# Router logits of a mixture-of-experts layer: standing router weights, tokens through four column groups, and a transpose back

## The reference

```python
h = tok(x, weight, weighted_sum)                      # (32, 512, 256)
h = h + attn(layernorm(h), ...)                       # ctx @ Wo + bo is its last step
xf = layernorm(h).reshape(-1, 256)
logits = xf @ router_w + router_b                     # router_w: (256, 8)
scores = softmax(logits, axis=-1)
G, idx = top_k(scores.T, 512)                         # per expert
...                                                   # experts on the chosen tokens, added into h
```

## Time and profile before

| what | value |
|---|---|
| median of 3 runs | 4833.21 us (4829.96 to 4833.23) |
| the profiled execution's own time | 4812.72 us |
| its span | 4811.0 us |
| mean granted TensorE clock | 0.959 of full |
| PE busy | 4480.2 us, 93% |
| DVE busy | 3479.2 us, 72% |
| ACT busy | 2664.6 us, 55% |
| POOL busy | 1843.0 us, 38% |

### The profile page before, as it was taken

The page is one execution under the profiler, slowest core; times in us unless marked ns, Lnnn a source line. Parts: engine busy times, 40 slices in busy tenths (PEclk is TensorE's granted clock), DMA queues, the critical chain, the costliest instruction groups (busy, mean ns, idle before and its releaser), DMA issues. The chain is left out here.

```text
span 4811.0 us, 92103 instructions
## 1 busy us (share of the span) xinstructions
PE 4480.2 (93%) x30324; PEld 3229.2 (67%) x30324; DVE 3479.2 (72%) x9091; ACT 2664.6 (55%) x5075; POOL 1843.0 (38%) x4431
## 2 busy tenths in 40 slices
PE   6999999699999999999999999999999997892699
PEld 5777777367776767766777766777767675772666
DVE  3333333288889888888899988889889896876411
ACT  1222222267777777777777777777777773440121
POOL 1222222244444444444444444444444442330032
PEclk9999999799999999999999999999999998995599
DMA  5888888899999999999999999999999995662033
GB/s 169 279 282 280 281 278 283 270 398 391 396 392 393 393 391 394 391 392 393 393 392 396 394 392 390 394 390 396 391 391 393 393 385 185 219 213 70 7 94 83
DMA packets 684020, 1540.36 MB, mean 320 GB/s; under 512 B 50211, under 2 KB 286163, under 8 KB 683475
## 3 DMA queue, kind: packets, MB, share of 16 engines
q1 hardware_dynamic: 674646, 1523.26, 85.7%
q0 software_dynamic: 6144, 8.52, 1.0%
q10 hardware_dynamic: 2816, 3.41, 0.3%
HBM read 753.82 MB, written 781.21 MB: 319 GB/s over the span
## 5 line engine op out<-in xcount | busy, mean ns | idle before, releaser
L984 ACT ACTIVATE a_probsT<-a_ps_m_t 128x512 f32<-128x512 f32 x2048 | 1228.4, 607 | 826.4 <-PE a_ps_m_t L924 826.4
L1046 DVE CUSTOM_DVE_ANT_1 a_scored<-a_ps_m_s,a_bias 128x512 f32<-128x512 f32 x2048 | 1397.7, 682 | 294.8 <-PE a_ps_m_s L915 283.1
L924 PE MATMUL a_ps_m_t<-a_ident,a_scored 128*128 128x128 f32 x8192 | 1256.6, 276 | 0.5 <-ACT a_probsT L984 0.5
L924 PEld LDWEIGHTS a_ps_m_t<-a_ident,a_scored 128*128 128x128 f32 x8192 | 934.7, 141 | 433.2 <-DVE a_scored L1053 431.2
L978 ACT ACTIVATE a_skew_in<-a_ps_m_tab 128x512 f32<-128x512 f32 x2048 | 1128.1, 617 | 67.7 <-PE a_ps_m_tab L901 36.1
L1053 DVE TENSOR_SCALAR a_scored<-a_scored,a_top_of 128x512 f32<-128x512 f32 x2048 | 1039.7, 527 | 0.0
L870 POOL TENSOR_SCALAR_AFFINE_SELECT a_bias<-a_bias 128x128 f32<-128x128 f32 (+2 forms) x2560 | 974.3, 407 | 35.1
L861 POOL COPY a_bias<-a_high 128x128 f32<-128x128 f32 (+1 forms) x1024 | 359.3, 380 | 1571.5 <-DMA a_bias<-d_skew 1571.5
L915 PE MATMUL a_ps_m_s<-a_ident,a_bias 128*128 128x128 f32 x5120 | 894.7, 273 | 0.0
L915 PEld LDWEIGHTS a_ps_m_s<-a_ident,a_bias 128*128 128x128 f32 x5120 | 688.7, 141 | 177.7 <-issue 1.0
L901 PE MATMUL a_ps_m_tab<-a_tabs,a_stack 128*128 128x256 bf16 x4096 | 709.3, 276 | 78.2 <-DMA a_ident<-in_ident 30.7
(11 more groups left out here) (195 smaller groups left out, 3658.2 us busy)
## 6 DMA issues: line engine op xcount, KB each, us to landing
d_skew<-a_skew_in SPq DMA_DIRECT2D x512, 1024.0 KB, 8.5
a_bias<-d_skew SPq DMA_DIRECT2D x512, 896.0 KB, 9.5
a_stack<-d_stack SPq DMA_DIRECT2D x256, 512.0 KB, 9.9
p_xt<-in_xT SPq DMA_DIRECT2D x31, 2048.0 KB, 10.4
d_stack<-p_extra SPq DMA_DIRECT2D x64, 512.0 KB, 3.2
d_ctx<-a_ctx_sb SPq DMA_DIRECT2D x128, 256.0 KB, 8.8
d_stack<-p_part_q SPq DMA_DIRECT2D x64, 384.0 KB, 2.8
d_stack<-p_part_k SPq DMA_DIRECT2D x64, 384.0 KB, 3.4
```

The lines of the kernel that those rows point to most:

```text
L924: mm = pe.transpose(m_t[:, k % 2, t * P:(t + 1) * P], scored[:, hh % SCORED, t, k * P:(k + 1) * P], ident[:])
L984: nc.scalar.activation(turned_at(hh // GH, hh % GH, k), m_t[:, k % 2], ACT.Exp, scale=SCALE).then_inc(turned, 1)
L1046: nc.vector.tensor_tensor_reduce(split(scored[:, hh % SCORED, t]), split(m_s[:, t % 2]), extra, 1.0, -3.0e38, ALU.add, ALU.max, top_of[:, ...
```

## The change

The router's weights are padded to 32 columns (`wr` is [128, 2, 32], cleared by POOL, and the load fills the first 8), and stand as weights; the tokens of one tile of 128 run through. The product of token tile t goes to the output partitions 32t to 32t+31, so that the logits come out with the experts on partitions and the tokens along the row (`by_expert`, 128x128). ACT copies that to SBUF (`logitsT`), PE transposes it (`turn_back`) into `by_token`, and DVE reads 8 of each 32 columns of it. `route(n)` moves ahead of `widen(n+3, 1)`, and `turn_back(n)` stands behind it.

```diff
@@ -1084,7 +1084,8 @@
 
     BUFS = 4
     ident, wo = sb("ident", [P, P]), sb("wo", [P, HC, H])
-    bo_row, wr, br_row = sb("bo_row", [P, H]), sb("wr", [P, HC, NE]), sb("br_row", [P, NE])
+    bo_row, wr, br_row = sb("bo_row", [P, H]), sb("wr", [P, HC, P // QT]), sb("br_row", [P, NE])
+    logitsT = sb("logitsT", [P, P])
     heads_f, heads = sb("heads_f", [P, OCT, HC, P]), sb("heads", [P, OCT, HC, P], BF16)
     minus_half = sb("minus_half", [P, QT])
     sums, inverse = sb("sums", [P, B // OCT, S]), sb("inverse", [P, S])
@@ -1096,17 +1097,18 @@
     xg, xT = sb("xg", [P, BUFS, QT, XG]), sb("xT", [P, HC, S])
     logits, expd = sb("logits", [P, QT, NE]), sb("expd", [P, QT, NE])
     top_of, total, share = sb("top_of", [P, QT]), sb("total", [P, QT]), sb("share", [P, QT])
-    m_o, m_turn, m_r = ps("m_o", [P, 2, QT, H]), ps("m_turn", [P, HC, S]), ps("m_r", [P, QT, NE])
+    m_o, m_turn, m_r = ps("m_o", [P, 2, QT, H]), ps("m_turn", [P, HC, S]), ps("m_r", [P, 2, QT, P // QT])
     m_share = ps("m_share", [P, S])
-    half_set, heads_in, heads_kept, wo_in, const_in = (
-        sem("o_" + n) for n in ("half_set", "heads_in", "heads_kept", "wo_in", "const_in"))
+    half_set, wr_cleared, heads_in, heads_kept, wo_in, const_in = (
+        sem("o_" + n) for n in ("half_set", "wr_cleared", "heads_in", "heads_kept", "wo_in", "const_in"))
     sums_in = [sem(f"o_sums_in{o}") for o in range(B // OCT)]
     c_loaded, h_loaded, h_stored, xg_stored = ([sem(f"o_{n}{u}") for u in range(BUFS)]
                                                for n in ("c_loaded", "h_loaded", "h_stored", "xg_stored"))
     (inverted, cut, share_done, scaled, o_done, h_added, h_done, st_done, mo_done, ve_done, rs_done, centred,
-     xn_done, turn_done, turned, r_done, soft, exp_done, xg_done) = (sem("o_" + n) for n in (
+     xn_done, turn_done, turned, routed, kept, r_done, soft, exp_done, xg_done) = (sem("o_" + n) for n in (
          "inverted", "cut", "share_done", "scaled", "o_done", "h_added", "h_done", "st_done", "mo_done", "ve_done",
-         "rs_done", "centred", "xn_done", "turn_done", "turned", "r_done", "soft", "exp_done", "xg_done"))
+         "rs_done", "centred", "xn_done", "turn_done", "turned", "routed", "kept", "r_done", "soft", "exp_done", "xg_done"))
+    by_expert, by_token = (m_r[:, k].rearrange("p t e -> p (t e)") for k in range(2))
     SOFT = 6
     CUTS = 5
     octets = B // OCT
@@ -1144,7 +1146,9 @@
             load_h(0)
             load_context(2)
             load_h(1)
-            for dst, src in ((ident[:], io["ident"]), (wr[:], io["router_w"].rearrange("(c p) o -> p c o", p=P)),
+            sp.wait_ge(wr_cleared, 1)
+            for dst, src in ((ident[:], io["ident"]),
+                             (wr[:, :, 0:NE], io["router_w"].rearrange("(c p) o -> p c o", p=P)),
                              (br_row[:], io["router_b"].partition_broadcast(P))):
                 sp.dma_start(dst, src).then_inc(const_in, 16)
             load_h(2)
@@ -1172,6 +1176,7 @@
 
         @block.gpsimd
         def _(pool):
+            nc.gpsimd.memset(wr[:], 0.0).then_inc(wr_cleared, 1)
             nc.gpsimd.memset(minus_half[:], -0.5).then_inc(half_set, 1)
             pool.wait_ge(half_set, 1)
             pool.wait_ge(wo_in, 32)
@@ -1230,11 +1235,16 @@
             def route(n):
                 after(pe, turned, HC * (n + 1))
                 after(pe, soft, SOFT * n)
-                for t in range(QT):
-                    for c in range(HC):
-                        mm = pe.matmul(m_r[:, t], xT[:, c, t * P:(t + 1) * P], wr[:, c], start=(c == 0),
-                                       stop=(c == HC - 1))
-                mm.then_inc(r_done, 1)
+                for c in range(HC):
+                    for t in range(QT):
+                        mm = pe.matmul(by_expert[t * (P // QT):(t + 1) * (P // QT)], wr[:, c],
+                                       xT[:, c, t * P:(t + 1) * P], start=(c == 0), stop=(c == HC - 1),
+                                       skip_group_check=True)
+                mm.then_inc(routed, 1)
+
+            def turn_back(n):
+                after(pe, kept, n + 1)
+                pe.transpose(by_token, logitsT[:], ident[:]).then_inc(r_done, 1)
 
             pe.wait_ge(heads_kept, 1)
             for n in range(3):
@@ -1251,9 +1261,10 @@
                     widen(n + 3, 0)
                 if n + 2 < B:
                     project_out(n + 2, n % 2)
+                route(n)
                 if n + 3 < B:
                     widen(n + 3, 1)
-                route(n)
+                turn_back(n)
 
         @block.scalar
         def _(act):
@@ -1278,8 +1289,11 @@
             for n in range(B):
                 for c in range(HC):
                     act.wait_ge(turn_done, HC * n + c + 1)
-                    after(act, r_done, n)
+                    after(act, routed, n)
                     nc.scalar.activation(xT[:, c], m_turn[:, c], ACT.Identity).then_inc(turned, 1)
+                act.wait_ge(routed, n + 1)
+                after(act, r_done, n)
+                nc.scalar.activation(logitsT[:], by_expert, ACT.Identity).then_inc(kept, 1)
                 act.wait_ge(soft, SOFT * n + 3)
                 nc.scalar.activation(expd[:], logits[:], ACT.Exp).then_inc(exp_done, 1)
                 if n + 2 < B:
@@ -1337,7 +1351,7 @@
                     after(dve, soft, SOFT * n + k)
 
                 after(dve, r_done, n + 1)
-                step(nc.vector.tensor_tensor(logits[:], m_r[:], br_row[:].unsqueeze(1).to_broadcast([P, QT, NE]),
+                step(nc.vector.tensor_tensor(logits[:], m_r[:, 1, :, 0:NE], br_row[:].unsqueeze(1).to_broadcast([P, QT, NE]),
                                              ALU.add), 1)
                 step(nc.vector.tensor_reduce(top_of[:], logits[:], AX.X, ALU.max), 2)
                 step(nc.vector.tensor_tensor(logits[:], logits[:], top_of[:].unsqueeze(2).to_broadcast([P, QT, NE]),
```

## The result

The changed kernel takes 4810.8 us in the median of 5 runs, the one before 4833.2 us: the ratio is 0.9956, with an interval of 0.9946 to 0.9967. That is 21 us or 0.44% faster (the two medians themselves lie 22.5 us apart). The two profiled executions, however, differ by only 7.7 us (4812.7 and 4805.0), close to the 6.6 us of the forecast's sum. One later execution of the changed kernel ran in a slower state of the chip (5246.6 us at a mean granted clock of 0.83) and one of before took 17821 us; neither is used for a reading.

A forecast was written before the change was run, and what follows sets the result against it. DVE and PE's 8.39 us ring bounds the output stage's batches, with 15.0 us lost to the clock. Ring 0, clock -3.9, tail -2.7 make -6.6 us: 4806, carried to the median as 4826.6 us, range 4816 to 4839.

The forecast's parts named there:

- the clock's term: Output stage's steady batches: half-clock losses of 15.0 us would become 11.1, a term of -3.9 us.
- the carrying over: Whole kernel: -6.6 us gave 4806 for the profiled execution; the median's 20 us above it was added, giving 4826.6.
- the floor of 239.3 us: Output stage's 27 steady batches without clock loss: 226.5 us at 8.39 each plus 12.8 us of DVE's in six batches.
- the tail: Last three batches, little overlap, half clock: the router product is on the path; the stage ends 2.7 us sooner.
- rival 1: The clock holds in the output stage: -13.8 us, about 4819; with no fall left -17.7, 4815.5. Chance 0.35.
- The ring of 8.39 us: Full-clock batch: share product, projection, DVE's addition of h, statistics and scaling set 8.39 us; the change shortens it by 0.
- The product's size: Router product on PE: its slot falls from 1.80 us to 0.58, so 1.2 us of PE a batch go.
- ACT's copy: Logits' 128x128 copy from PSUM: 0.37 us, lying where ACT stands still for 3.87 us before the exponential.
- the transpose back: PE's transpose of the logits behind the second share product: 0.13 us, hidden under DVE's 0.68 us scaling.
- the order's hand-overs: Router product first: PE waits 0.7 us for ACT's copies; the second share product still ends 1.1 us early. Nothing lost.
- The clock, as a mechanism: A share product between router product and transposes removes most regular falls (two left, 1.65 us each); six long batches fall, 1.3 each.
- the six long ones: Steady batches where DVE also does the reciprocal (three, 10.77 us) or its cutting up (three, 10.28); 7.8 us clock loss forecast.

The follow-up runs named there:

- the later comparison: The changed kernel, nothing edited, run again beside the form alone on one chip: 4810.5 us, 0.9964 of before.
- the form alone: The changed kernel with the router product back at its old place behind the second share product: 4803.0 us (0.9954); repeated, 4800.4 us (0.9944).
- both kernels with filler: Idle 128x128 by 256-column bf16 products before the first share product: 7 (14 in long batches) in the change, 4804.0 us; 4 in before, 4821.3 us.
- the order alone: The kernel before with only its old router product moved ahead of the second share product: 4836.5 us, 1.0023 of before.
- the dense idle products: The form alone plus 8 idle products of 128x128 by 256 bf16 columns behind the router product: 4808.5 us, 0.9966 of before.
- The weak and the dense products: Weak: the form alone plus 4 idle products of the old router product's shape, 4817.4 us (0.9982). Dense: the dense idle products, 4808.5 us.

## Why the prediction was wrong, by its own steps

**The step that failed** is the size of the clock's term, and with it the carrying over. The prediction took the 15.0 us that one execution loses to the clock as the kernel's ("The other 15.0 are the clock"), let 11.1 stand in their place (-3.9), and wrote: "The median of the runs shown is 4833.2, 20 us more than the profiled one; carried over, 4826.6". The 20 us between the profiled execution and the median were not an even shift. The execution of 4830.8 us has 18 of them: 4 ahead of the stage (4021.2 against 4017.3) and 14 in it (356.2 against 342.0). Over the floor of 239.3 us the three profiled executions of before lose 15.0, 21.0 and 28.7 us; the change's loses 10.2. Taken from the third of them, the clock's term is -18.5 us, not -3.9. With the tail that makes -20.6, and 21 us were measured. The range failed with it: rival 1 was bounded by the same 15.0 ("If no fall is left at all, -17.7: 4815.5"). That the median stood 20 us over the profile, in a kernel where I held the clock for the unsure term, was the sign that should have widened it.

How well -20.6 fits is partly luck. The two executions behind it took 4830.8 and 4805.0 us: 21.1 of their 25.8 us are in the stage, 5.4 ahead of it, where nothing was changed. The change's is the fastest of its five, 5.7 us under their median, and no execution of it at its median was profiled. In the later comparison, where before had a median of 4825.1 us, the change gained 17 us by the ratio (15 between the medians). With the profile of 4823.5 us in the third one's place the clock's term is -10.8 us. So against ordinary executions of before the term is known as some -11 to -19 us; against the first profile it is -4.8, close to what was forecast.

**The ring of 8.39 us** was right for the change: it stands unchanged there, in the form alone and in both kernels with filler, and 44 us less of PE's work in the steady part (229.5 to 185.9) bought nothing by themselves. It does not stand in the order alone, nor in the last batches with the dense idle products.

**The product's size, ACT's copy, the transpose back and the order's hand-overs** were right: 0.65 us, 0.28 for 0.37, no wait of DVE, waits of 0.74 and 1.01. The stage outside of its steady part is 85.6 us for 87.7, -2.1 for the forecast's -2.7, but not as the sum had it: behind the steady part it is 36.8 us for 40.4, so the tail gave 3.6, and ahead of it 48.8 for 47.3 to 47.9, so that the start, put at nothing, costs 1 us or a little more (48.5 in the form alone). Why it does was not tested. The product's slot in the earlier trace rows was 0.58 us and is 0.58 us here (4201.72 to 4202.30, the next share product). The Trainium skill ("TensorEngine Tiling (Array Packing)", Tiling Modes, Key Properties) states that a change of tiling mode drains TensorE. This trace shows no cost of it beyond those 0.58 us.

**The clock, as a mechanism,** was half right. Falls in regular batches gone, falls in the six long ones over the projection: so it came, with 10.2 us where I had 11.1 (1.7 each for 1.3, the upper end of the prediction's own span, and none in regular batches for two; the two misses nearly cancel). The reason was wrong: the order does not do it. The new order alone costs time: 8 us in the old form (4836.5 against 4828.3), 9 to 10 in the new one.

**What gives the time** lies in two places. *The chains.* They are 19.4 of the 28.7 us of before's third profile, and all that the change wins by the clock against it. They are gone with the shorter product at either place, and they are gone with the old product untouched and dense idle products in the stretch behind it. PE's waits alone don't make them, since waits of about 1 us before the first share product bring none in the change and in the form alone; nor do 0.9 us of the old product's shape put back behind the new one. What in the old stretch does make them is not shown further than that. *The long batches.* Before loses 9.3 us there in that profile and the change 10.2, so the change as made wins nothing in them; at the old place the new form loses 1.1 and 3.2. With half of the old product's time put back in its own shape it is 18.9 us, and the kernel takes 4817.4 us in place of 4800.4 to 4803.0 (on other chips). The weak and the dense products, of equal length at half clock, show a part of the reason: behind the weak ones the clock comes back later, and PE is the late engine. Why the chip lets the clock fall after one stretch and not after another, and gives it back sooner in one than in another, none of these runs says.

## What to carry to other kernels

A profile is one execution. Where its own time lies 0.4% from the median, find which stage has the difference before taking any loss in it as the kernel's; a second and a third profile of the unchanged kernel show it. Compare like with like: the best fit of a sum to a measurement is worth little when the two executions behind it stand differently to their medians. An engine off the ring is not free if its clock follows its work: time saved on it shows when the clock is at half and it would be the late one. And when something is moved, look at what stays behind it in the rare long batches, not in the regular ones: the better version here is the new product at the old place, 10 us faster than the change.

## What the runs showed of the hardware that was not expected

The spread. Executions of before lie between 4813 and 4837 us, those of the form alone between 4798 and 4806. In the three profiles of before 14 of 18 us of it are in one stage of some 350 us, most of that in how many of its regular batches chains of the clock's falls run over; 4 us are ahead of it. What decides how many chains an execution gets, none of the traces says.

A second rhythm at full clock. In the last batches of the kernel with dense idle products the logits' steps came so late against POOL that DVE's subtraction (L1365) met POOL's addition (L1187). In the full-clock batch of before the subtraction (L1343) starts at 4207.27 and POOL's addition at 4207.38, 0.11 us behind it; here the addition is first, by 0.08 us:

```profile
4279.06 2.35 POOL L1187 TENSOR_TENSOR o_h_in<-o_h_in,o_bo_row 128x1024 f32<-128x1024 f32 x1
4279.14 2.32 DVE L1365 TENSOR_TENSOR o_logits<-o_logits,o_top_of 128x32 f32<-128x32 f32 x1
...
4281.50 0.23 ACT L1306 ACTIVATE o_expd<-o_logits 128x32 f32<-128x32 f32 x1 [3.58 <-DVE o_logits L1365]
```

It took 2.32 us where it takes 0.19 otherwise; ACT's exponential, its scaling of the next batch, the copies and the router product followed later, and the batches stayed at some 9.1 us in place of 8.39 to the end of the steady part. What pushed the steps there is not shown; DVE waits 0.22 us for the transpose back in two of these batches. In regular batches of before, the change, the form alone and before with filler, it is a later product (L1348 in before) that takes 1.52 to 1.55 us beside POOL's addition, and DVE still waits 0.7 us for the projection behind it.
